# Attention stage of a four-layer graph network: remainders and third words formed for two steps at once, interleaved values in a ring of six, run masks made in the dense passes

## What is computed

```
h = x @ W
alpha = x_i @ wa[:c] + edge_attr @ wa[c:c + ce] + x_j @ wa[c + ce:]
alpha = where(alpha > 0, alpha, 0.2 * alpha)
m = segment_max(alpha, dst)
a = exp(alpha - m[dst])
s = segment_sum(a, dst)
out = segment_sum((a / (s[dst] + 1e-16))[:, None] * h[src], dst) + bias
x = layernorm(x + out)
```

## Time and profile before

| what | value |
|---|---|
| median of 3 runs | 3594.78 us (3585.97 to 3599.09) |
| the profiled execution, its own time | 3591.77 us |
| span of its profile | 3590.0 us |
| busy, share of the span: PE, DVE, ACT, POOL | 81%, 81%, 62%, 44% |
| TensorE's granted clock, mean | 0.94 of full |
| HBM traffic over the span | 251 GB/s |

### The profile page before, as it was taken

The page is one execution under the profiler, slowest core; times in us unless marked ns, Lnnn a source line. Parts: engine busy times, 40 slices in busy tenths (PEclk is TensorE's granted clock), DMA queues, the critical chain, the costliest instruction groups (busy, mean ns, idle before and its releaser), DMA issues.

```text
span 3590.0 us, 122167 instructions
## 1 busy us (share of the span) xinstructions
PE 2911.7 (81%) x50473; PEld 2637.4 (73%) x50473; DVE 2904.2 (81%) x4610; ACT 2219.8 (62%) x6003; POOL 1584.4 (44%) x1253
## 2 busy tenths in 40 slices
PE   0199999999999699899688888787768888888886
PEld 0178888888888599899677777777757777777775
DVE  7599999999999522233688888898857999999997
ACT  6334444444444400001698888898857898899887
POOL 2012222222221000000399988898964655666564
PEclk9999999999999899999899999999977888888887
DMA  8157777777777799898687877787738888888884
GB/s 221 66 157 244 237 232 234 243 237 231 234 243 236 253 370 360 330 328 320 215 279 259 264 264 248 254 271 250 257 124 302 279 278 277 276 290 274 267 278 129
DMA packets 606666, 907.43 MB, mean 253 GB/s; under 512 B 358505, under 2 KB 494858, under 8 KB 587163
## 3 DMA queue, kind: packets, MB, share of 16 engines
q1 hardware_dynamic: 583992, 800.62, 68.1%
q10 hardware_dynamic: 19763, 94.38, 7.1%
q0 software_dynamic: 2352, 4.52, 0.3%
HBM read 651.96 MB, written 247.40 MB: 251 GB/s over the span
## 4 chain that ended last, share of the span: by engine, by line
PE 36%; DVE 27%; ACT 14%; issue 10%; POOL 6%; DMA 5%; ACTq 1%; SPq 0%; DVEq 0%; POOLq 0%
PE ps L683 9%; PE ps L1047 8%; PE ps L709 4%; DMA U<-AD 4%; ACT U L1627 3%; POOL EDG L1268 3%; DVE EDG L1755 3%; DVE U L1817 3%; PE ps L696 3%; ACT U L569 3%; POOL EDG L1260 2%; ACT U L1329 2%; PE ps L667 2%; PE ps L1289 1%; DVE A L1389 1%
## 5 line engine op out<-in xcount | busy, mean ns | idle before, releaser
L569 ACT ACTIVATE U<-ps 128x512 bf16<-128x512 f32 (+1 forms) x637 | 356.4, 573 | 499.5 <-PE ps L696 475.5
L1627 ACT ACTIVATE U<-U,T 128x65 f32<-128x65 f32 x1806 | 460.1, 343 | 47.7 <-PE ps L1688 42.3
L1260 POOL TENSOR_TENSOR EDG<-U,edge 128x512 f32<-128x512 f32 (+1 forms) x196 | 214.3, 1098 | 584.1 <-DVE edge L1412 551.1
L1047 PE MATMUL ps<-U 128*128 128x192 bf16 x4802 | 418.5, 248 | 33.2 <-DMA U<-AD 32.8
L1047 PEld LDWEIGHTS ps<-U 128*128 128x128 bf16 x4802 | 402.8, 98 | 42.5 <-DMA U<-AD 39.2
L1655 POOL TENSOR_TENSOR U<-U 128x455 f32<-128x455 f32 x258 | 296.4, 1152 | 215.3 <-DVE U L1817 215.3
L866 DVE TENSOR_TENSOR EDG<-edge,EDG 128x1792 bf16<-128x1792 bf16 x343 | 367.5, 1083 | 14.4 <-DMA OSD<-EDG 12.0
L502 POOL DMA_INDIRECT U<-REC,nod x49 | 94.0, 1918 | 622.4 <-PE ps L638 501.2
L683 PE MATMUL ps<-U 128*128 128x98 bf16 (+1 forms) x5292 | 363.5, 223 | 4.5 <-DVE U L854 3.5
L709 PE MATMUL ps<-EDG,U 128*128 128x193 bf16 x2401 | 311.4, 249 | 51.1 <-ACT U L569 39.9
L683 PEld LDWEIGHTS ps<-U 128*128 128x128 bf16 x5292 | 341.3, 98 | 15.7 <-DVE U L854 11.9
(11 more groups left out here) (323 smaller groups left out, 7019.4 us busy)
## 6 DMA issues: line engine op xcount, KB each, us to landing
U<-ROWS SPq DMA_DIRECT2D x411, 448.0 KB, 4.7
U<-AD SPq DMA_DIRECT2D x98, 1568.0 KB, 8.6
OND<-EDG SPq DMA_DIRECT2D x343, 224.0 KB, 2.8
OSD<-EDG SPq DMA_DIRECT2D x343, 224.0 KB, 3.6
AD<-U ACTq DMA_DIRECT2D x49, 1568.0 KB, 5.6
EDG<-ROWS SPq DMA_DIRECT2D x171, 448.0 KB, 6.3
U<-OND SPq DMA_DIRECT2D x303, 224.0 KB, 5.9
U<-OSD SPq DMA_DIRECT2D x213, 224.0 KB, 4.7
```

The costliest lines, as they stand in the source:

```text
L569: ev4.by(act.activation(prow[i % NPW][:, P * g:P * (g + m)], ps[4 + gg % 2][:, 0:P * m], ACT.Copy))
L1047: ins = pe.matmul(ps[q][:, 0:192], arow[r][:, P * j:P * j + P], (XsB if p else XsA)[:, j, :, :].rearrange("p s f -> p (s f)"), start=(j == ...
L1260: ins = pool.tensor_tensor(VD[:, v:v + w, 0, KA * D:G * D].rearrange("p w (k f) -> p w k f", f=D), W_, bc(c_.unsqueeze(3), [P, w, G - KA, ...
L1627: ins = act.activation(V4[k % NV][:, 0, c, :], H[k % NHR][:, c, :], ACT.Copy, scale=a4[d % 2][:, s:s + 1])
```

## The change

1. `V4`, three planes a tile in a ring of four, becomes `VR`: six tiles of 455 pairs of f32. A pair's first f32 is the value, the second the remainder, and the third word is a bf16 that GpSimd puts into the lower half of the remainder. `VS` is the same memory as bf16; PE reads elements 1 to 3 of each four. ACT's products (L1627) now go to every second f32.
2. DVE forms the remainders of two steps in one instruction of 910 elements, at odd k; GpSimd the third words of two steps likewise. PE's scatter moves from offset 19 to 20, the sum of a block and the last norm from 26 to 27, the loop is one step longer.
3. PE's transposition, ACT's copy and GpSimd's four instructions for the masks leave the attention loop. A new `passes_pool` makes the masks of all 49 blocks during the dense passes, 7 blocks at a time, from destinations that SP loads ahead of the first row of AD (ROWS3, 49 x 6272 bf16, 614656 bytes), and SP stores them in the second pass (7 stores, together 49 x 49 x 2 x 128 bf16, 1229312 bytes). The attention loop loads them, one transfer of 49 x 256 bf16 for each block. One small f32 transposition of PE becomes a bf16 matmul.
4. The ring `odp` keeps its 17 tiles, of which some move.

The helpers `value_at` and `rest_at` wait for a step's value as before, since GV and GR are empty.

```diff
...
+        msk_ld, msk_st = on(rw_st[0], 32 * ((NB + 1) // 2)), on(rw_st[1], 32 * (NB // 2))
+        msk_ok, msk_d = on(rec_t, NB), on(rank_ok, 2 * NB)
+        mdst = EDG[0:NB, 0:3136].bitcast(BF16)[:, 0:NB * P].rearrange("p (d r) -> p d r", r=P)
+        mboth = EDG[0:NB, 3136:9408].bitcast(BF16).rearrange("p (d m r) -> p d m r", m=2, r=P)
+        mdif = U[0:NB, upper + NB * 96:upper + NB * 96 + GB * 129].rearrange("p (d r) -> p d r", r=129)
+
+        def passes_pool(pool):
+            msk_d.by(pool.memset(mdif[:, :, 0:1], 1.0))
+            msk_d.by(pool.memset(mdif[:, :, P:P + 1], 1.0))
+            pool.wait_ge(msk_ld.at, msk_ld.o + 16)
+            for g in range(NGB):
+                bl = slice(GB * g, GB * g + GB)
+                if g:
+                    pool.wait_ge(msk_ok.at, msk_ok.o + 2 * g)
+                    msk_d.by(pool.memset(mdif[:, :, 0:1], 1.0))
+                    msk_d.by(pool.memset(mdif[:, :, P:P + 1], 1.0))
+                msk_d.by(pool.tensor_tensor(mdif[:, :, 1:P], mdst[:, bl, 1:P], mdst[:, bl, 0:P - 1], ALU.subtract))
+                pool.wait_ge(msk_d.at, msk_d.o + 4 * g + 3)
+                msk_d.by(pool.tensor_scalar(mdif, mdif, 0.0, 1.0, ALU.is_equal, ALU.subtract))
+                pool.wait_ge(msk_d.at, msk_d.o + 4 * g + 4)
+                msk_ok.by(pool.tensor_scalar(mboth[:, bl, 0, :], mdif[:, :, 0:P], BIG, None, ALU.mult))
+                msk_ok.by(pool.tensor_scalar(mboth[:, bl, 1, :], mdif[:, :, 1:P + 1], -1.0, None, ALU.mult))
+            pool.wait_ge(msk_st.at, msk_st.o + 16 * NGB)
+
         def passes_sp(sp):
+            msk_ld.by(sp.dma_start(mdst, ROWS3[1].rearrange("d (s r) -> s d r", r=P)), 16)
...
+                    if p and i % GB == GB - 1:
+                        g = i // GB
+                        sp.wait_ge(msk_ok.at, msk_ok.o + 2 * g + 2)
+                        msk_st.by(sp.dma_start(MSK[GB * g:GB * g + GB].rearrange("d s m r -> s d (m r)"),
+                                               mboth[:, GB * g:GB * g + GB, :, :].rearrange("p d m r -> p d (m r)")), 16)
...
+            sp.wait_ge(msk_st.at, msk_st.o + 16 * NGB)
...
-        LASTT = NT + 27 + 15
+        LASTT = NT + 28 + 15
...
-        NV = 4
-        vparts = [part(o4 + 1365 * i, 1365) for i in range(NV - 1)] + [MISC[:, 0:1365]]
-        V4 = [v.rearrange("p (s k f) -> p s k f", s=3, f=65) for v in vparts]
-        S4 = [v.bitcast(BF16).rearrange("p (s k f h) -> p s k f h", s=3, f=65, h=2)[:, :, :, :, 1] for v in vparts]
-        o4 += 1365 * (NV - 1)
+        NV, NE = 6, G * 65
+        VR = part(o4, NV * NE * 2).rearrange("p (v e w) -> p v e w", v=NV, w=2)
+        VS = part(o4, NV * NE * 2).bitcast(BF16).rearrange("p (v e h) -> p v e h", v=NV, h=4)
+        o4 += NV * NE * 2
...
-        odp = [part(o4 + 448 * i, 448) for i in range(15)] + [Aflat[:, a4o + 1792:a4o + 2240], Tflat[:, 2700:3148]]
-        o4 += 15 * 448
+        odp = [part(o4 + 448 * i, 448) for i in range(11)] + [Aflat[:, a4o + 1792:a4o + 2240], Tflat[:, 2700:3148], Tflat[:, 1225:1673]] \
+            + [MISC[:, 448 * i:448 * i + 448] for i in range(3)]
+        o4 += 11 * 448
...
-        seg, negs, lastf, ylast = (Tflat[0:NB, 1225 + 130 * n:1225 + 130 * n + w] for n, w in enumerate((129, P, P, P)))
+        ylast = Tflat[0:NB, 2267:2267 + P]
+        masks = [MISC[0:NB, 1365 + P * i:1365 + P * i + P].bitcast(BF16).rearrange("p (m r) -> p m r", m=2) for i in range(2)]
+        identh = ident[0:NB, 0:NB].bitcast(BF16).rearrange("p (r h) -> p r h", h=2)[:, :, 1]
...
+            def run_masks(d):
+
+                if d >= 2:
+                    sp.wait_ge(ytr.at, ytr.o + d - 1)
+                mk_ld[d % 2].by(sp.dma_start(masks[d % 2], MSK[d]), 16)
+
...
+            run_masks(0)
+            run_masks(1)
...
-                d = block4(t, 40)
+                d = block4(t, 2)
+                if d is not None and d >= 2:
+                    run_masks(d)
+                d = block4(t, 41)
...
-                        act.wait_ge(vok.at, vok.o + k - NHR + 1)
+                        value_at(act, k - NHR)
...
-                d = block4(t, 6)
-                if d is not None:
-                    act.wait_ge(dtr.at, dtr.o + d + 1)
-                    if d:
-                        act.wait_ge(flg.at, flg.o + 2 * d)
-                    dcp.by(act.activation(dcol, ps[2][0:NB, P:2 * P], ACT.Copy))
...
-                if k is not None:
+                if k is not None and g not in GV:
...
-                        ins = act.activation(V4[k % NV][:, 0, c, :], H[k % NHR][:, c, :], ACT.Copy, scale=a4[d % 2][:, s:s + 1])
+                        ins = act.activation(VR[:, k % NV, 65 * c:65 * c + 65, 0], H[k % NHR][:, c, :], ACT.Copy, scale=a4[d % 2][:, s:s + 1])
...
-                d = block4(t, 37)
+                d = block4(t, 38)
...
         def pairs4_pool(pool):
...
-                d = block4(t, 7)
-                if d is not None:
-                    pool.wait_ge(dcp.at, dcp.o + d + 1)
-                    if d == 0:
-                        pool.wait_ge(pre_d.at, G + 1)
-                    if d:
-                        pool.wait_ge(ylok.at, ylok.o + d)
-                        pool.wait_ge(ytr.at, ytr.o + d)
-                        pool.wait_ge(flg.at, flg.o + 2 * d)
-                    sgk.by(pool.tensor_tensor(seg[:, 1:P], dcol[:, 1:P], dcol[:, 0:P - 1], ALU.subtract))
-                    pool.wait_ge(sgk.at, sgk.o + 2 * d + 1)
-                    sgk.by(pool.tensor_scalar(sege, seg, 0.0, 1.0, ALU.is_equal, ALU.subtract))
-                    pool.wait_ge(sgk.at, sgk.o + 2 * d + 2)
-                    flg.by(pool.tensor_scalar(negs, sege[:, 0:P], BIG, None, ALU.mult))
-                    flg.by(pool.tensor_scalar(lastf, sege[:, 1:P + 1], -1.0, None, ALU.mult))
...
-                if k is not None:
-                    pool.wait_ge(rok.at, rok.o + k + 1)
-                    look.by(pool.tensor_tensor(V4[k % NV][:, 2, :, :], V4[k % NV][:, 1, :, :], S4[k % NV][:, 1, :, :], ALU.subtract))
+                if k is not None and (k % 2 or k == NG - 1):
+                    v, w = (k - k % 2) % NV, 1 + k % 2
+                    pool.wait_ge(rok.at, rok.o + k // 2 + 1)
+                    look.by(pool.tensor_tensor(VS[:, v:v + w, :, 2], VR[:, v:v + w, :, 1], VS[:, v:v + w, :, 3], ALU.subtract))
...
         def pairs4_pe(pe):
...
-                d, g, k = due4(t, 19)
+                d, g, k = due4(t, 20)
...
-                    pe.wait_ge(look.at, look.o + k + 1)
+                    pe.wait_ge(look.at, look.o + k // 2 + 1)
...
-                        ins = pe.matmul(ps[6 + d % 2][:, 0:195], ODn[k % NOD][:, c, :], S4[k % NV][:, :, c, :],
+                        ins = pe.matmul(ps[6 + d % 2][:, 0:195], ODn[k % NOD][:, c, :], VS[:, k % NV, 65 * c:65 * c + 65, 1:4],
...
-                d = block4(t, 5)
-                if d is not None:
-                    if d:
-                        pe.wait_ge(dcp.at, dcp.o + d)
-                    dtr.by(pe.transpose(ps[2][0:NB, P:2 * P], E3v[:, d, :, 1], ident[:, :]))
...
-                    pe.wait_ge(flg.at, flg.o + 2 * d + 2)
...
-                    ytr.by(pe.transpose(ps[3][:, 64:64 + NB], lastf, ident[0:NB, 0:NB]))
+                    ytr.by(pe.matmul(ps[3][:, 64:64 + NB], masks[d % 2][:, 1, :], identh, start=True, stop=True))
...
-                if k is not None:
-                    dve.wait_ge(vok.at, vok.o + k + 1)
-                    rok.by(dve.tensor_tensor(V4[k % NV][:, 1, :, :], V4[k % NV][:, 0, :, :], S4[k % NV][:, 0, :, :], ALU.subtract))
+                if k is not None and (k % 2 or k == NG - 1):
+                    v, w = (k - k % 2) % NV, 1 + k % 2
+                    value_at(dve, k)
+                    rok.by(dve.tensor_tensor(VR[:, v:v + w, :, 1], VR[:, v:v + w, :, 0], VS[:, v:v + w, :, 1], ALU.subtract))
...
-                    dve.wait_ge(flg.at, flg.o + 2 * d + 2)
-                    dvf.by(dve.tensor_tensor_scan(ysc, negs, ps[2][0:NB, 0:P], -BIG, ALU.add, ALU.max))
+                    dve.wait_ge(mk_ld[d % 2].at, mk_ld[d % 2].o + 16 * (d // 2 + 1))
+                    dvf.by(dve.tensor_tensor_scan(ysc, masks[d % 2][:, 0, :], ps[2][0:NB, 0:P], -BIG, ALU.add, ALU.max))
...
-                    ylok.by(dve.tensor_tensor(ylast, ysc, lastf, ALU.mult))
+                    ylok.by(dve.tensor_tensor(ylast, ysc, masks[d % 2][:, 1, :], ALU.mult))
...
-                d = block4(t, 26)
+                d = block4(t, 27)
...
-                    redd.by(dve.tensor_reduce(A[:, d % NA4, 0:65], ps[6 + d % 2][:, 0:195].rearrange("p (s f) -> p f s", f=65), AX, ALU.add))
-                last_norm(t - 26)
+                    redd.by(dve.tensor_reduce(A[:, d % NA4, 0:65], ps[6 + d % 2][:, 0:195].rearrange("p (f s) -> p f s", s=3), AX, ALU.add))
+                last_norm(t - 27)
...
         def again(s):```

```

(1 more changed line is left out.)

21 lines of the change are left out of this document (17 added, 4 removed).

## The result

The changed kernel takes **3686.1 us** (median of 4 runs, 3684.3 to 3691.9); the kernel before, run beside it, takes 3593.4 (3586.0 to 3599.1). The ratio is 1.0262, 95% interval 1.0249 to 1.0275: **93 us slower**, where 38 us less were forecast. The time lies outside the range.

A forecast was written before the change was run, and what follows sets the result against it. DVE, partly waiting for GpSimd on a shared path, was taken to set the pace, ACT close behind. Attention loop -48, given back +6 and +2.5, dense passes +1.5: -38 us from 3594.8 gives 3557 us, range 3508 to 3610.

The forecast's parts named there:

- Given back: Loads on SP behind `odp` tiles freed a step later: target rows cost 6 us, 0 to 30; the extra loop step 2.5.
- The pairs of third words: GpSimd in the attention loop: 1.70 us per 910 elements, 5.95 us a block; DVE waits 1.0 us a block less, 0 to 2.8.
- 36% less of the common path: GpSimd's third words and masks fall from 9.3 to 5.95 us a block; DVE's waiting of 2.8 us falls in proportion.
- longer holds: Rival: DVE waits in fewer but longer pieces, its 2.8 us a block stay; about 3590 us, chance 0.13.
- The floor of 3517: Rival: all DVE's waiting goes and ACT paces the attention loop at 15.7 us a block; 3517 us, counted within the forecast's 0.70.
- The ring of six: ACT's wait for PE to free a value tile, about 1.3 us a block, mostly goes; no gain by itself.
- half-rate rival: Rival: DVE's interleaved remainders run at 1.8 ns an element, costing 2.5 us a block; about 3680 us, chance 0.07.
- two-byte stores at 4.2 us: Rival: GpSimd's third-word stores cost what ACT pays, 4.2 us per 910 elements; 240 us more, 3830 us, chance 0.10.
- The pairs of remainders: DVE in the attention loop: 3.5 instructions fewer a block, about 80 ns each, gain 0.28 us a block; at worst 2.5 lost.
- the waiting fell: Sign: L1788 and L1783 at means of 0.8 to 0.9 us show less DVE waiting for GpSimd; 0.95 or more would not.

The follow-up runs named there:

- masks_alone: The kernel before with the run masks made in the dense passes, ring of four and planar tiles kept: 3572.6 us beside 3586.6 (0.9961).
- before_ring_of_16: The kernel before with one one-hot tile less in the ring `odp` (16 for 17), nothing else: 3648.4 us beside 3586.6 (1.0177).
- interleaving_alone: Kernel before with masks in the dense passes, plus interleaved value tiles, still four, old offsets, nothing in pairs: 3597.3 us beside 3588.8 (1.0020).

## Why the prediction was wrong

The parts as the runs separate them, in us a block (x 49 for the time):

| kernel | us | a block | this step |
|---|---|---|---|
| before | 3588 | 17.48 | |
| + masks in the dense passes | 3572.6 | 16.91 | -0.57 |
| + interleaved tiles | 3597.3 | 17.41 | +0.50 |
| + ring of six, PE at 20, `hots` at 4 | 3597.8 | 17.46 | +0.05 |
| + remainders in pairs | 3569.9 | 16.96 | -0.50 |
| + third words in pairs | 3604.0 | 17.65 | +0.69 |
| + `hots` at 3 again: the change | 3686.1 | 19.25 | +1.60 |

(Of before, the median beside these runs, 3587 to 3594.) The steps are measured in this order only, and a block is that of one execution each, so times and blocks don't match to the last us. They differ most in the first step: 0.57 x 49 = 28 us against 14 by the medians. The stage starts 5 us later with the masks, and the profile of before is of an execution of 3591.8 us, 5 above the median beside *masks_alone*.

**The step that failed: "Given back".** It saw the mechanism (PE frees a tile of `odp` a step later, target rows are queued on SP behind it, L1755 already waits) and priced it at 6 us, 0 to 30. It measured 82 us (77 by the ratios). I held the landing time of one load against its slack and multiplied by the loads concerned. But SP goes through its list in order: where it stands at the ring's wait in most steps (210 waits in about 255 steps), it hardly works ahead, and each late load puts DVE back, DVE the small work, PE, and so the ring that SP stands at. This circle is read from the waits and the order of time; what the runs test is that the loss comes with SP's place behind PE and goes with it. The profile of before held the warning, and I hadn't read it: SP was already 204.6 us of 700 at that wait, the largest of its three. The *before_ring_of_16* run priced one step of that slack at 62 us.

**The pairs of third words** were mis-sized in two ways. The instruction takes 2.26 us, not 1.70: of the unknown two-byte store I took "nothing" or ACT's price (4.2 us), and the truth is 0.5 us above the lower end. So the forecast's base, 36% less of the common path, was about 15%: (6.6 + 2.75 - 7.9) / 9.35. And the sign was wrong. I named longer holds as a rival with nothing gained (3590); the runs show a loss of 0.69 us a block. It isn't a longer waiting of DVE in sum (2.6 us a block in pairs, 2.5 step by step): the waiting falls on a chain of small instructions (L1888, 1.56 us for 49 elements), and PE gets the first tile of a pair later, for which the prediction had no term. How much is which stays open. The Trainium skill's lock rule (SBUF — State Buffer, Who interferes with whom), cited for that rival, agrees with the trace: with GpSimd's work left out DVE's tiles take 0.67 to 0.68 us each.

**Waiting isn't time.** The forecast let a fall of DVE's waiting count in full, up to ACT's pace. With all of it taken away the block gained 0.81 us, where the waiting on the tiles of 1792 alone had been (1030-680) x 143 + (949-670) x 57 + (897-670) x 57 + (929-670) x 29 ns = 86 us in 700, 2.1 a block. The rest went into waits for target rows and for ACT. The floor of 3517 was near: 3526.9.

**The ring of six** did what was said (ACT's wait for the scatter, 35.3 us in 700 on tiles in U and 16.0 on the one in MISC, is 2.9 us in the whole changed run) and gave nothing: ACT waits for PE's gather instead, 110.8 us in 700. The interleaving that made room for it cost 0.50 us a block that I priced at nothing. PE's scatter from interleaved tiles, 275 for 254 ns, wasn't in the sum at all; GpSimd's dearer store was, as a rival. Which of the two makes the 0.50, the runs don't part.

**Right:** L1851 at 1.10 us, so the half-rate rival is false, though its 3680 is near the result; two-byte stores at 4.2 us are false too. The pairs of remainders gained, more than priced. Inside the dense passes the pace is as before (434.6 us of PE in 1240 to 1720 us, 437.2 before), but their start is later:

```profile
1252.25 3.93 PE L1078 MATMUL ps<-U 128*128 128x192 bf16 x25 [18.89 <-DMA U<-AD]
```

PE starts 3.5 us later (1248.75 in the earlier trace rows), after a wait of 18.89 us against 14.78; forecast were 1.7 us, 3.5 at most. The check I had written ("DVE's wait for target rows above 10 us in 700 would show loads that come late") named the right row; its price was what failed. Another sign misled: L1788 and L1783 have means of 0.83 and 0.67 us, as low as I wanted for "the waiting fell", in a kernel that lost 93 us, since DVE stood idle for rows and the waiting sat on L1888.

## What to carry to other kernels

When an edit makes a ring's tile come free a step later, look first at the in-order queue that waits for it: how long the queue already stands there, and what is queued behind. If it is there in most steps, move that load one step down the list or add a tile, before anything else of the change is judged. Before two steps' work is merged into one instruction, look at who takes the first step's result and at what small work meets the longer hold: here the same merge gained 0.50 us a block on DVE and lost 0.69 on GpSimd. And change one thing at a time: the masks alone were worth 14 us, and the rest of the change hid that.

## What the runs showed of the hardware

- GpSimd, 910 elements: reading f32 at every eighth byte costs nothing (1.705 us); storing two bytes at every eighth takes 2.23 to 2.40 us (medians of the two forms) against 1.80 side by side; storing four bytes at every eighth 1.96 at the median, 1.71 at best.
- PE, moving operand of 65 x 3 bf16 words: taken as three of the four halves of every eight bytes, a matmul of 195 columns shows 274 ns for 254 from three planes (minima 271 and 251), and seven in a row 0.94 us for 0.80. Between *masks_alone* and *interleaving_alone* the layout of this operand and the order of the columns changed, and where some one-hot tiles lie.
- TensorE's granted clock: after a wait of 3.01 us it was 0.51 (1.2 GHz) for 12 us and 21 matmuls of 65 columns took 1.34 us for 0.84 at full clock.
- A DVE instruction of 49 elements, 0.25 us alone, took 1.56 us on average behind GpSimd's 2.26 us.
- DVE runs a subtraction of interleaved f32 at full rate: 1.09 us at the minimum for 910 elements, where 1.03 ns an element and the fixed part gave 1.10.
